# An attention and feed-forward layer on eight cores: two maxima formed on partition 64 instead of partition 0, without a transfer between the two

## What is computed

```python
xn = layernorm(x)
latent = xn @ Wc_down                    # 1024 -> 512
q = (latent @ Wq_up)                     # 16 heads of 64
k, v = split(latent @ Wkv_up)            # one head of 64, shared by all 16
att = softmax(causal(q @ k.T / sqrt(64)))
s = (att @ v) @ Wc_proj
g = silu(ffn(xn))                        # ffn: silu(gate) * up, then down; int weights / 127
out = x + s * g
```

## Time and profile before

| what | us |
|---|---|
| run 1, run 2 | 3245.21, 3211.35 |
| median of the two | 3228.28 |
| profiled execution, whole | 3203.96 |
| its spans, fastest to slowest core | 3173.9 to 3202.3 |
| PE busy, share of the span of the slowest core | 2065.4 (64%) |
| ACT busy | 1305.9 (41%) |
| DVE busy | 1166.7 (36%) |
| PEld busy | 989.3 (31%) |
| POOL busy | 418.1 (13%) |

### The profile page before, as it was taken

The page is one execution under the profiler, slowest core; times in us unless marked ns, Lnnn a source line. Parts: engine busy times, 40 slices in busy tenths (PEclk is TensorE's granted clock), DMA queues, the critical chain, the costliest instruction groups (busy, mean ns, idle before and its releaser), DMA issues.

```text
span 3202.3 us, 32980 instructions; the slowest of 8 cores (3173.9 to 3202.3 us)
## 1 busy us (share of the span) xinstructions
PE 2065.4 (64%) x10424; PEld 989.3 (31%) x10464; DVE 1166.7 (36%) x1850; ACT 1305.9 (41%) x1457; POOL 418.1 (13%) x329
## 2 busy tenths in 40 slices
PE   1333545466575584785858758597575887578885
PEld 1112323222342341442225322253221442223521
DVE  4634443243433535424243251423422421511221
ACT  0111232222332342433634437344465437476465
POOL 0211122323243011101101001100111001011011
PEclk7556767777798797997879968799787898799988
DMA  5022264939677254351015300163001260012510
GB/s 96 29 48 50 42 97 56 153 69 156 69 81 132 53 125 123 76 152 35 28 44 128 109 22 21 42 139 100 14 18 44 63 165 21 23 28 54 147 33 14
DMA packets 547286, 232.12 MB, mean 72 GB/s; under 512 B 476464, under 2 KB 532784, under 8 KB 547120
## 3 DMA queue, kind: packets, MB, share of 16 engines
q1 hardware_dynamic: 429792, 186.88, 22.5%
q0 software_dynamic: 117328, 43.14, 12.7%
HBM read 241.62 MB, written 27.26 MB: 84 GB/s over the span
## 4 chain that ended last, share of the span: by engine, by line
PE 40%; DVE 20%; DMA 13%; ACT 11%; issue 10%; POOL 5%; DVEq 1%; SPq 1%; ACTq 0%; POOLq 0%
PE ps_sc L566 9%; PE ps_y L553 9%; ACT p_sb L577 9%; PE ps_u L724 5%; PE ps_u L731 5%; POOL p_sb L585 4%; PE ps_u L795 4%; DVE recbf L605 3%; DMA wu_t<-wu 3%; DMA xt<-xb 3%; PE ps_u L643 2%; DVE stat L303 2%; DVE h_sb L742 2%; DVE xnT L377 2%; DMA wd_t<-wd 1%
## 5 line engine op out<-in xcount | busy, mean ns | idle before, releaser
L577 ACT ACTIVATE p_sb<-ps_sc 128x1024 bf16<-128x1024 f32 x1088 | 1087.7, 1022 | 1326.1 <-PE ps_sc L566 1319.7
L553 PE MATMUL ps_y<-p_sb,vaug_sb 128*65 128x512 bf16 x2176 | 731.5, 421 | 245.9 <-POOL p_sb L585 144.2
L566 PE MATMUL ps_sc<-qs,kT_sb 65*128 65x512 bf16 x2176 | 734.2, 422 | 20.4 <-DVE qs L534 20.4
L585 POOL TENSOR_TENSOR p_sb<-p_sb,masks_sb 128x1024 bf16<-128x1024 bf16 x128 | 278.3, 2184 | 2251.1 <-ACT p_sb L577 2250.8
L553 PEld LDWEIGHTS ps_y<-p_sb,vaug_sb 128*65 128x65 bf16 x2176 | 210.2, 119 | 676.2 <-issue 597.7
L370 PE MATMUL ps_u<-ident_sb,xn_t 128*128 128x128 bf16 x512 | 65.3, 271 | 417.0 <-DVE xn_t L333 238.5
L566 PEld LDWEIGHTS ps_sc<-qs,kT_sb 65*128 65x128 bf16 x2176 | 219.9, 106 | 227.3 <-issue 82.2
L724 PE MATMUL ps_u<-xnT_own,wg_t 128*128 128x256 bf16 x1536 | 222.1, 293 | 92.9 <-DVE h_sb L742 71.4
L795 PE MATMUL ps_u<-wd_t,h_sb 128*128 128x512 bf16 x744 | 193.0, 397 | 79.2 <-DVE o_sb L813 31.4
L595 DVE CAST yf<-ps_y 64x1024 bf16<-64x1024 f32 x32 | 38.8, 1214 | 559.6 <-PE ps_y L553 559.6
L731 PE MATMUL ps_u<-xnT_own,wu_t 128*128 128x256 bf16 x1536 | 220.4, 291 | 16.2 <-DMA wu_t<-wu 14.6
(11 more groups left out here) (84 smaller groups left out, 1225.3 us busy)
## 6 DMA issues: line engine op xcount, KB each, us to landing
wg_t<-wgbf SPq DMA_DIRECT2D x144, 256.0 KB, 3.5
wu_t<-wubf SPq DMA_DIRECT2D x144, 256.0 KB, 3.8
wd_t<-wdbf SPq DMA_DIRECT2D x288, 128.0 KB, 2.7
xt<-xb SPq DMA_DIRECT2D x64, 512.0 KB, 4.4
wg_t<-wg POOLq DMA_DIRECT2D x48, 256.0 KB, 7.4
wu_t<-wu POOLq DMA_DIRECT2D x48, 256.0 KB, 8.3
wd_t<-wd POOLq DMA_DIRECT2D x96, 128.0 KB, 5.2
xo_t<-xo SPq DMA_DIRECT2D x16, 512.0 KB, 4.5
```

Of the source, the lines that this page charges most:

```text
L553: last = O("tensor", lambda e_, t=t, nh=nh, par=par: e_.matmul(ps_y[0:65, nh * 512:(nh + 1) * 512], vaug_sb[:, t, :], p_sb[:, par, nh * 51 ...
L566: sct = O("tensor", lambda e_, t=t, nh=nh, sb2=sb2: e_.matmul(ps_sc[:, sb2 * 1024 + nh * 512:sb2 * 1024 + (nh + 1) * 512], kT_sb[0:65, t * ...
L577: ex = O("scalar", lambda e_, sb2=sb2: e_.activation(p_sb[:, sb2, :], ps_sc[:, sb2 * 1024:(sb2 + 1) * 1024], AF.Exp), [sct, st["p_war"][sb ...
L585: mtoks[t] = O("gpsimd", lambda e_, pview=pview, mj=mj: e_.tensor_tensor(pview, pview, masks_sb[:, mj, :].unsqueeze(1).broadcast_to([128, ...
```

## The change

A new constant tile `b64_sb` of 65 columns holds 0 in the columns 0 to 63 and 1 in column 64. It replaces the column of ones as the stationary operand of the two summing matmuls (lines 449 and 498). The sums then come out on partition 64 of `ps_u`, and zeros on partitions 0 to 63, which nobody reads. Both maxima, the running maximum, the product and the square root move to partition 64, with the same operations. The DMA to `mrow` goes, with SP's wait for the scalar. Line 534 reads the scalar from `q2m` directly; the condition for overwriting `q2m` is line 534's end instead of the DMA's. Two memsets at the start are added.

```diff
+    b64_sb = sbuf("b64_sb", [128, 65], BF16)
...
+        tb64 = O("vector", lambda e: e.memset(b64_sb[:, :], 0.0), out="v")
+        O("vector", lambda e: e.memset(b64_sb[:, 64:65], 1.0), [tb64], out="v")
...
             k2m = O("tensor", lambda e: e.matmul(
-                ps_u[0:1, 128:384], ones_sb[0:64, 0:1], sc_bf[0:64, 0:256],
+                ps_u[0:65, 128:384], b64_sb[0:64, 0:65], sc_bf[0:64, 0:256],
                 start=True, stop=True), [sqk, vaev, t_consts], out="mm")
...
-            r1 = O("vector", lambda e: e.reduce_max(stat[0:1, 21:22], ps_u[0:1, 128:384],
+            r1 = O("vector", lambda e: e.reduce_max(stat[64:65, 21:22], ps_u[64:65, 128:384],
...
-                    ps_u[0:1, half * 512:(half + 1) * 512], ones_sb[:, 1:2],
+                    ps_u[0:65, half * 512:(half + 1) * 512], b64_sb[:, 0:65],
                     sc_bf[:, :], start=True, stop=True), [qsq], out="mm"))
...
-            m1 = O("vector", lambda e_: e_.reduce_max(q2m[0:1, 0:1], ps_u[0:1, 0:1024],
+            m1 = O("vector", lambda e_: e_.reduce_max(q2m[64:65, 0:1], ps_u[64:65, 0:1024],
...
-            md = O("sync", lambda e_, e=e: e_.dma_start(
-                mrow[64:65, e:e + 1], q2m[0:1, 4:5]), [m4], out=f"md{e % 2}", dma=True)
-            st["q2m_war"] = md
...
                 ones_sb[64:65, 2:3].broadcast_to([1, QS_W]),
-                mrow[64:65, e:e + 1]), [md, evn, t_consts, st["qs_war2"][qpar]], out="v")
+                q2m[64:65, 4:5]), [m4, evn, t_consts, st["qs_war2"][qpar]], out="v")
+            st["q2m_war"] = aug
             aug_done[e] = aug
```

More of the change, by code:

```diff
@@ L449, in gen_kv_block @@
             k2m = O("tensor", lambda e: e.matmul(
-                ps_u[0:1, 128:384], ones_sb[0:64, 0:1], sc_bf[0:64, 0:256],
+                ps_u[0:65, 128:384], b64_sb[0:64, 0:65], sc_bf[0:64, 0:256],
                 start=True, stop=True), [sqk, vaev, t_consts], out="mm")
             st["scbf_war"] = k2m
-            r1 = O("vector", lambda e: e.reduce_max(stat[0:1, 21:22], ps_u[0:1, 128:384],
+            r1 = O("vector", lambda e: e.reduce_max(stat[64:65, 21:22], ps_u[64:65, 128:384],
                                                     axis=AX.X), [k2m, st["lnmax"]], out="v")
-            r2 = O("vector", lambda e: e.tensor_tensor(stat[0:1, 20:21], stat[0:1, 20:21],
-                                                       stat[0:1, 21:22], ALU.max), [r1], out="v")
+            r2 = O("vector", lambda e: e.tensor_tensor(stat[64:65, 20:21], stat[64:65, 20:21],
+                                                       stat[64:65, 21:22], ALU.max), [r1], out="v")
             st["lnmax"] = r2
@@ L520, in emit_latq_m @@
             (evn,) = latq_ctx.pop(e)
-            m2 = O("vector", lambda e_: e_.tensor_tensor(q2m[0:1, 1:2], q2m[0:1, 0:1],
-                                                         stat[0:1, 20:21], ALU.mult),
+            m2 = O("vector", lambda e_: e_.tensor_tensor(q2m[64:65, 1:2], q2m[64:65, 0:1],
+                                                         stat[64:65, 20:21], ALU.mult),
                    [st["lnmax"], latq_ctx2.pop(e)], out="v")
             st["lnmax"] = m2
[L525 to L528, removed]
+            m3 = newton_rsqrt_ap(m2, q2m[64:65, 1:2], q2m[64:65, 2:3], q2m_i[64:65, 0:1],
+                                 q2m[64:65, 3:4], iters=1)
+            m4 = O("vector", lambda e_: e_.tensor_tensor(q2m[64:65, 4:5], q2m[64:65, 1:2],
+                                                         q2m[64:65, 2:3], ALU.mult),
                    [m3, st["q2m_war"]], out="v")
-            md = O("sync", lambda e_, e=e: e_.dma_start(
-                mrow[64:65, e:e + 1], q2m[0:1, 4:5]), [m4], out=f"md{e % 2}", dma=True)
-            st["q2m_war"] = md
             qpar = e % 2
```

## The result

The changed kernel takes 3177.82 us in the median of 11 runs (3166.28 to 3199.31), the kernel before 3214.94 in the median of 10 (3202.96 to 3269.4). The ratio is 0.9887 with a 95% interval of 0.9854 to 0.9920, a gain of 1.1% or some 36 us. The ratio leaves out executions in which the cores of a die ran at a lower clock, and the medians, which differ by 37 us, include them.

What follows compares the result with a forecast made beforehand. No single engine bounds the kernel; a hand-written order of four engines handing work on does. 9.0 + 14.9 + 9.0 - 2.6 = 30.3 us off 3211.35 gives 3181, predicted as 3180 us, range 3150 to 3213.

Steps and rivals of the forecast that it cites:

- Early barriers: Places 0 to 2 of the 16 line-534 multiplies: tile loads leave before the scalar, reduction 3.0 us earlier each, 9.0 us.
- Long stalls: Places 3 and 4, the feed-forward's first pass: waits of 10.25 and 11.65 us, partly given back to weight loads, 14.9 us gained.
- Place 5: Transfer of `yT` stands behind six write-backs that wait for loads, not for the scalar: 0 gained, at most 6.8 us.
- Places with a feed-forward step: Places 6, 7, 8, 10, 12, 14: line 738 starts 1.5 us earlier and TensorE takes all of it, 9.0 us.
- Attention-only places: Places 9, 11, 13, 15: TensorE's attention work hides all of the DMA, 0 gained; without that cover 6.8 us in all.
- The 65 columns: 64 one-column matmuls at lines 449 and 498: longer weight loads cost 2.6 us, ends 0 and 7.6.
- Given back wholly: Rival: places 3 and 4 bring nothing, the weight stream alone sets the pass's end; gain 15.4 us, 3196; chance 0.20.
- Doesn't show: Rival: each place's gain is taken up by the next wait of the static order; 3211 to 3218 us; chance 0.06.
- slower: Rival: VectorE's steps move onto GpSimd's mask multiplies, 3.8 us each; 8 to 12 meetings give 3211 to 3227; chance 0.04.
- The GpSimd row: Evidence for the slower rival: line 290 took 3.96 us, to the end of a GpSimd multiply that ran for 4.24 us.
- Everything counts: Rival: the weight stream isn't bound by its pace and nothing covers the rest; gain 47.7 to 54.5 us, 3160; chance 0.17.

Runs made afterwards that it cites:

- e2: The changed kernel with the scalar's DMA put back at places 3 and 4 alone; 0.9918 of the kernel before, about 10 us slower than the changed kernel.
- e8: The changed kernel with VectorE held by two small memsets (1.85 us expected, no DMA) before line 534 at places 6 to 15; 0.9918 of the kernel before.
- e3: The changed kernel with VectorE held by eight memsets before line 534 at places 6, 7, 8, 10, 12, 14; 1.0079 of the kernel before.
- e4: The changed kernel with VectorE held by eight memsets before line 534 at places 9, 11, 13, 15; 0.9978 of the kernel before.

## Why the prediction was right, step by step

The predicted time was 3180, the measured one 3177.8; the gain was forecast at 30.3 us and measured at 36 by the ratio, 37 by the medians. That the times agree within 2 us is luck: the base, 3211.35, lay 3.6 us under the median of the kernel before, and with a rounding by 1 that hid most of the 6.8 us by which the gain was too small. The parts are further off than the sum: the early barriers and the stalls were put 1.7 and 2.2 us too high, the two later kinds of places 3.7 and 5.5 too low, and 2.6 were taken off for the columns.

- **Early barriers.** The mechanism came as described: loads ahead of the scalar, the reduction 1.57 us behind it instead of 4.55. The reduction gained the 3.0 us forecast on core 6 (3.3 to 3.6 in the mean of the cores), but the stretches only 2.2 to 2.5. Some 1 us each is taken by later waits; which is open.
- **Long stalls.** The step that mattered, that part of each stall is given back to the weight stream, held in size: 6.2 against 6.4 forecast and 6.5 against 8.5, of 10.15 and 11.55 us of VectorE's time, and e2 confirms it with the DMA put back. The path was as forecast, TensorE waiting for weights, behind place 4 alone: in the next 45 us it waits 7.9 to 9.1 us for `wu_t` in the kernels without the DMA and 3.9 to 4.5 in those with it (means of the cores). Behind place 3 it does not wait for weights at all. There GpSimd does, whose queue issues the converting loads: the next load needs the buffer, and the buffer needs its write-back (no such wait with the DMA, 3.0 to 3.9 us without). The mask multiplies stand behind that issue, and TensorE waits for them, 6.5 to 7.2 us against 2.7 to 2.8. Changed kernel, core 6, timeline:

```profile
401.64 0.87 POOL L692 DMA_DIRECT2D wu_t<-wu  x1 [1.61 <-DMA wubf<-wu_t]
402.53 4.19 POOL L586 TENSOR_TENSOR p_sb<-p_sb,masks_sb 128x1024 bf16<-128x1024 bf16 x2
...
404.80 1.03 PE L554 MATMUL ps_y<-p_sb,vaug_sb 128*65 128x512 bf16 x2 [3.82 <-POOL p_sb L586]
```

  The second stall was sized by core 6, where the write-backs on either side of it are 14.75 us apart (548.60 to 563.35); in the mean of the cores it is 12.95. The pace of 6.3 us per pair held (6.3 before, 6.4 in the changed kernel). The stretch repeats only within 4 us, so the miss of 2 is not beyond its noise.
- **Place 5.** Nothing, as argued from SP's write-backs: 0.3.
- **Places with a feed-forward step.** Mis-sized: 12.7 for 9.0. TensorE's next instruction came 1.6 to 2.0 us earlier at the five places from 7 on, and 3.3 at place 6, where the wait had been longer; that is 11.8 in all. The clock comes on top: at the sixth exponential behind the scalar the six places have gained 16.4 us, of which 12.7 are left at the next place. The windows before (core 6, place 14) and after at the same distance from the scalar:

```profile
2531.00:2536.00 5.00, 4.64 (x21) 2.62 (x22) 1.71 (x3) 1.45 (x2) 0.00 (x0) 0.66 0.22 48
```

```profile
2488.46:2493.46 5.00, 3.96 (x27) 2.56 (x28) 1.62 (x4) 2.26 (x3) 0.00 (x0) 1.00 0.55 126
```

  The kernel before had the clock at 0.66 behind the wait, the changed kernel at 1.00. In the same window of all six places on the eight cores it was 1.00 in 5 of 48 with the DMA, in 47 of 48 without, and in 7 of 48 in e8, which has no DMA and holds VectorE alone. The sum had priced a wait at its length. By e3 and e8 its price at these places is more: 9.6 us for 7.95 held, 2.8 for about 1.85 at places 7, 8, 10, 12, 14.
- **Attention-only places.** Here a step failed: "the cover is TensorE's attention work, and it hides all of the DMA". The places gained 5.5 us in all. I had read one core, 6, at one place, 11, where TensorE's line 613 came late. At that place seven of the eight cores show the same cover; at 9, 13 and 15 only two, three and one do. On the other 19 of the 32 core-places VectorE did not wait for line 613 at all, and the multiply was what came last. e4 shows the size: of 7.95 us held 7.6 counted, where the forecast's cover would have left 5.3. Line 617 itself came 0.5 to 0.8 us earlier in the mean, and with it the projection behind the transfer of `yT`, 0.6 to 0.9 us: that is the path of e4's row at the DMA's own length. How the rest of each 1.4 us arises stays open; place 11, covered on seven cores, still gained 1.1.
- **The 65 columns.** The loads are longer, by 29 ns, where the prediction's rows gave 40 and the rule of the Trainium skill that it cites gives 53; the measurement decides. No cost shows: the idle times in front of the query matmuls and of the reduction behind them are the same. The term of 2.6 us should have been its lower end, 0, though the total can't part the two.
- **The rivals.** "Given back wholly" is out (e2, and the stretches). "Doesn't show" and "slower" are out. (The GpSimd row is two multiplies of 2.1 us, not one of 4.24.) "Everything counts" was nearer for places 6 to 15 than the forecast, and wrong for places 3 to 5.

## What to carry to other kernels

In a static order over several engines, price a wait at each place by what stands behind it in the same engine's order, and read every place of a kind, on several cores: a cover seen at one place may be missing at the others. A transfer of four bytes was waited for 1.7 us where nothing was in its queue and 10 to 12 where it stood behind transfers that wait for others; computing a value on the partition where it is needed removes both, and here the wider matmul that does so had no cost that showed. Where a queue issues loads and computes as well, what a stall gives back can come through it, as GpSimd's masks did here. Before moving a load earlier, see whether it is the load that ends the wait: here a 6.5 us operation on one partition did, and giving TensorE other work behind it and moving that operation was worth more than the change studied.

## What the runs showed of the hardware

- An idle time of 1.7 us in TensorE was followed by a granted clock of 0.66 over the next 5 us where the same stretch without it had 1.00 (below 1.00 in 43 of 48 core-places with the wait, in 1 of 48 without); after 8.3 us of idleness it was 0.50, and came back to 0.87 in the 5 us that began 5.6 us later. A wait of VectorE can so cost more than its length: 57.6 us for 47.7 held.
- Dependent memsets of VectorE of 0.72 us each started 1.02 us apart, with 0.29 us idle between them, where other dependent small steps start 0.10 us behind the end of the last (174.86 + 0.15 to 175.12).
- A weight load of 65 columns took 108 ns against 79 for one column in the same place (medians), and the matmul's idle time did not grow. One of 128 columns took 97 ns (line 724, kernel before).
- GpSimd's queue is held by the issue of a load whose buffer isn't free: 3.0 to 3.9 us behind place 3, and TensorE waited 6.5 to 7.2 us for the mask multiplies that stand behind it, against 2.7 to 2.8 where that issue wasn't held.
